# Minus the maximum from one product of four 32-row tiles, and a pair's denominators from one product of four 32-column tiles

## What is computed

```python
q = (c_q @ w_up_q.T).reshape(b, s, H, DH).transpose(0, 2, 1, 3)
k = (c_kv @ w_up_k.T).reshape(b, s, H, DH).transpose(0, 2, 1, 3)
q, k = _apply_rope_subspace(q, DR), _apply_rope_subspace(k, DR)
scores = jnp.einsum('bhqd,bhkd->bhqk', q, k) * scale
attn = jax.nn.softmax(scores, axis=-1)
out = jnp.einsum('bhqk,bhkd->bhqd', attn, v)      # v = c_kv @ w_up_v.T
out = out @ w_out.T + residual
```

## Time and profile before

| | us |
|---|---|
| median of 3 runs | 938.64 |
| fastest and slowest of them | 935.33, 938.98 |
| the profiled execution | 931.6 |
| its span | 929.6 |
| PE busy in the span | 822.2 (88%) |
| DVE busy | 664.6 (71%) |
| POOL busy | 633.4 (68%) |
| ACT busy | 384.8 (41%) |

### The profile page before, as it was taken

One profiled execution on the slowest core, in us unless ns is written; L12 is line 12 of the kernel. 1 busy time (PEld: TensorE's weight loads), 2 busy tenths in 40 slices (PEclk: granted clock), 3 DMA queues, 4 the chain that ended last, 5 costly groups with the idle time before them and its releaser, 6 DMA issues.

```text
span 929.6 us, 14668 instructions
## 1 busy us (share of the span) xinstructions
PE 822.2 (88%) x5118; PEld 493.0 (53%) x5118; DVE 664.6 (71%) x1198; ACT 384.8 (41%) x622; POOL 633.4 (68%) x324
## 2 busy tenths in 40 slices
PE   3555799999999999999999999999999979859681
PEld 2323555555555555555555555555555435448681
DVE  7897877777777777777777777777777776646022
ACT  2203354444444444444444444444444434316350
POOL 3201897878878787878787878787877777432433
PEclk8757799999999999999999999999999999879796
DMA  7200000101010101111010111010010000058693
GB/s 201 65 0 1 12 13 13 25 13 24 13 24 13 25 13 25 26 22 24 13 24 13 24 14 24 13 24 14 13 13 13 13 13 13 12 185 268 214 332 85
DMA packets 84328, 43.88 MB, mean 47 GB/s; under 512 B 57632, under 2 KB 73376, under 8 KB 84192
## 3 DMA queue, kind: packets, MB, share of 16 engines
q1 hardware_dynamic: 83232, 40.86, 17.2%
q0 software_dynamic: 1024, 2.10, 0.8%
HBM read 36.51 MB, written 6.16 MB: 46 GB/s over the span
## 4 chain that ended last, share of the span: by engine, by line
PE 75%; DVE 13%; DMA 4%; issue 2%; POOL 2%; ACT 1%; SPq 1%; POOLq 0%; DVEq 0%
PE ps_o L428 24%; PE ps_m L394 8%; PE ps_x L382 8%; PE ps_s L412 6%; PE ps_s L414 6%; PE ps_s L418 6%; PE ps_s L416 6%; PE ps_s L443 3%; DVE mx L941 3%; DMA moe<-xs_dram 2%; PE ps_s L436 2%; POOL xs_dram L808 2%; PE ps_s L547 1%; PE ps_s L538 1%; DVE hn L878 1%
## 5 line engine op out<-in xcount | busy, mean ns | idle before, releaser
L794 POOL TENSOR_TENSOR acc<-acc,probs 128x1024 f32<-128x1024 f32 (+1 forms) x192 | 460.1, 2396 | 83.2 <-ACT probs L633 61.4
L941 DVE TENSOR_REDUCE mx<-ps_m 128x2 f32<-128x1024 f32 x240 | 293.6, 1223 | 91.6 <-PE ps_m L394 91.1
L633 ACT ACTIVATE probs<-ps_s 128x1024 f32<-128x1024 f32 x256 | 249.2, 1024 | 165.1 <-PE ps_s L418 165.1
L428 PE MATMUL ps_o<-probs,c_all 128*64 128x512 f32 x1024 | 249.7, 609 | 0.0
L394 PE MATMUL ps_m<-k_hi,q_hi 64*128 64x512 f32 x480 | 108.3, 446 | 11.0 <-issue 6.6
L794 POOL TENSOR_TENSOR acc<-probs 128x1024 f32<-128x1024 f32 (+1 forms) x32 | 75.4, 2355 | 58.8 <-ACT probs L633 58.3
L412 PE MATMUL ps_s<-q_hi,k_hi 64*128 64x512 f32 x512 | 103.8, 401 | 11.9 <-DVE x_sb L1005 11.9
L428 PEld LDWEIGHTS ps_o<-probs,c_all 128*64 128x64 f32 x1024 | 62.4, 137 | 93.0 <-issue 43.6
L414 PE MATMUL ps_s<-q_hi,k_lo 64*128 64x512 f32 x512 | 102.7, 396 | 0.0
L418 PE MATMUL ps_s<-neg_row,one_row 64*128 64x512 f32 x512 | 102.1, 393 | 0.0
L416 PE MATMUL ps_s<-q_lo,k_hi 64*128 64x512 f32 x512 | 102.0, 393 | 0.0
(11 more groups left out here) (264 smaller groups left out, 1018.5 us busy)
## 6 DMA issues: line engine op xcount, KB each, us to landing
probs<-in_experts SPq DMA_DIRECT2D x15, 578.0 KB, 5.8
rr<-rd_dram SPq DMA_DIRECT2D x62, 128.0 KB, 3.1
wu<-in_wqk SPq DMA_DIRECT2D x16, 256.0 KB, 3.3
neg_row<-nm SPq DMA_DIRECT2D x256, 0.5 KB, 2.0
w_first<-in_experts SPq DMA_DIRECT2D x5, 578.0 KB, 4.4
rot<-in_experts SPq DMA_DIRECT2D x5, 578.0 KB, 5.7
hT<-in_experts SPq DMA_DIRECT2D x5, 578.0 KB, 5.6
xs_dram<-zero SPq DMA_DIRECT2D x2, 960.0 KB, 6.5
```

The lines of the kernel that those rows point to most:

```text
L428: ins = nc.tensor.matmul(ps_o[64 * h:64 * h + 64, :], c_all[:, (p // HP) * TB + kt, :], probs[:, st % 4, h, :], start=(kt == 0), stop=(kt ...
L633: nc.scalar.activation(probs[:, st % 4, :, :], ps_s[:, 2 * (st % 2):2 * (st % 2) + 2, :], ACT.Exp, scale=SCALE).then_inc(s["probs"], 1)
L794: V.tensor_tensor(acc[:, half, heads, :], first, probs[:, st % 4, heads, :], ALU.add).then_inc(s["added"], 1)
L941: V.reduce_max(mx[:, :, kh, qt], max_banks(q, n), AX.X).then_inc(s["max_reduced"], 1)
```

## The change

Four things are done at once.

1. `less_max(p, g)` comes ahead of the two scores of a group: four matmuls on 32-row tiles (partitions 0, 32, 64, 96), one for each head and step, into the four banks of `ps_s`, which start the accumulation that `score` goes on with. `score` loses its fourth product. `one_row` has ones in four partitions, and `neg_row` minus the maxima of head 0 on partitions 0 and 32 and of head 1 on 64 and 96, so `max_rows` has 16 copies for each half instead of 8. As `less_max` writes all four banks it waits for the probabilities of the step just before, and in group 0 for both output sums of the pair before, in group 4 for the read of the denominators.
2. `denominators(p - 1, (0, 1))` makes both halves of a pair at once, with four 32-column tiles, in group 3 of pair p, ahead of `pv`, into bank 0. `acc` and `ou` get a third buffer so that half 0 can wait.
3. Behind it everything of a pair is done once: one read by ScalarE, four copies in `den_cols`, one `recip`, one `inv_rows`, four copies in `inv_spread`, two `divide` at the end of group 6, both `outputs` in group 7 ahead of `pv` (banks 0 and 1), and both `out_add` at the end of group 7.
4. The last pair keeps two separate halves at its end.

```diff
+            def less_max(p, g):
+                half = g // 4
+                ge(pe, s["probs"], n_step(p, 2 * g) - 1)
+                if g % 4 == 0:
+                    pe.wait_ge(row_placed[half], 256 * (p + 1))
+                if g == 0:
+                    ge(pe, s["out_added"], 2 * (p - 1))
+                if g == 4:
+                    ge(pe, s["den_read"], n_den(p - 1))
+                for h in range(2):
+                    for odd in range(2):
+                        j = quarter(2 * h + odd)
+                        nc.tensor.matmul(ps_s[:, 2 * odd + h, :], one_row[j, :],
+                                         neg_row[j, p % 2, half * HALF:(half + 1) * HALF], start=True, stop=False)
...
-                for h in range(2):
-                    ins = nc.tensor.matmul(bank[h], one_row[rows(h), :], neg_row[rows(h), p % 2, qc], start=False, stop=True)
...
+            def denominators(p, halves, bank):
+                for half in halves:
+                    wait_adds(pe, p, TB * half + TB - 1)
+                    for h in range(2):
+                        ins = nc.tensor.matmul(bank[quarter(2 * half + h), :], ones[:, 0:32], acc[:, buf(p, half), h, :],
+                                               start=True, stop=True)
...
@@ PE, in the loop over groups, behind up() @@
+                    if p > 0 and g in (3, 7):
+                        pe.wait_ge(s["probs"], n_step(p, 2 * g))
+                        if g == 3:
+                            denominators(p - 1, (0, 1), ps_s[:, 0, :])
+                        else:
+                            outputs(p - 1, 0, ps_s[:, 0, :])
+                            outputs(p - 1, 1, ps_s[:, 1, :])
@@ DVE, in the loop over groups @@
-                    if g == 0 and p >= 2:
-                        out_add(p - 2, 1, ps_s[:, 3, :])
-                    if g == 4 and p >= 1:
-                        out_add(p - 1, 0, ps_s[:, 3, :])
+                    if g == 5 and p > 0:
+                        recip(p - 1)
                     if p < LAST:
                         reduce_max(p + 1, 2 * g)
...
-                        if g in (0, 4):
-                            recip(p - 1, g // 4)
-                        if g in (2, 6):
-                            divide(p - 1, g // 4)
+                        if g == 6:
+                            divide(p - 1, 0)
+                            divide(p - 1, 1)
+                        if g == 7:
+                            out_add(p - 1, 0, ps_s[:, 0, :])
+                            out_add(p - 1, 1, ps_s[:, 1, :])
@@ SP, max_rows @@
-                for h in range(2):
+                for j in range(4):
+                    h = j // 2
                     for n in range(4):
-                        row = neg_row[64 * h:64 * h + 1, ...]
+                        row = neg_row[32 * j:32 * j + 1, ...]
@@ SP, in the loop over pairs @@
-                    den_cols(p - 1, 0)
-                    inv_rows(p - 1, 0)
-                    inv_spread(p - 1, 0)
                 if p < LAST:
                     max_rows(p + 1, 0)
                 if p > 0:
-                    den_cols(p - 1, 1)
-                    inv_rows(p - 1, 1)
-                    inv_spread(p - 1, 1)
+                    den_cols(p - 1, (0, 1))
+                    inv_rows(p - 1, (0, 1))
+                    inv_spread(p - 1, (0, 1))
```

More of the change, by code:

```diff
@@ L200, in build @@
             "added_last": "the same for head 1 of the last pair's second half (vector)",
-            "den_product": "half a pair's denominators (tensor)",
-            "den_read": "and read (scalar)",
-            "inverses": "denominators inverted (vector)",
+            "den_product": "a pair's denominators; half of the last pair's (tensor)",
+            "den_read": "and read (scalar, the last half vector)",
+            "inverses": "and inverted (vector)",
             "sums_copied": "latent sums of half a pair are in SBUF (scalar)",
@@ L268, in n_part, with n_den, buf, quarter @@
             return 2 * p + half + 1
+        def n_den(p, half=0):
+            return p + 1 + (half if p == LAST else 0)
+        def buf(p, half):
+            return (2 * p + half) % 3
+        def quarter(j):
+            return slice(32 * j, 32 * j + 32)
         def n_unit(q, u):
@@ L411, in score @@
                 for h in range(2):
-                    nc.tensor.matmul(bank[h], k_hi[rows(h), p % 3, kc], q_hi[rows(h), p % 3, qc], start=True, stop=False)
+                    nc.tensor.matmul(bank[h], k_hi[rows(h), p % 3, kc], q_hi[rows(h), p % 3, qc], start=False, stop=False)
                 for h in range(2):
@@ L506, in _ @@
                             pv(p - 1, NSTEP + n)
[L507 to L518, removed]
             pv(LAST, NSTEP - 2)
             pv(LAST, NSTEP - 1)
-            pe.wait_ge(s["den_read"], n_part(LAST, 0))
-            denominators(LAST, 1, ps_x[:])
+            pe.wait_ge(s["den_read"], n_den(LAST))
+            last_denominators(ps_x[:])
             def slots_T(i, k):
@@ L1250, in max_rows @@
                     sp.wait_ge(s["scores"], n_step(q - 2, TB * half + TB - 1))
[L1251 removed]
+                for j in range(4):
+                    h = j // 2
                     for n in range(4):
[L1253 removed]
+                        row = neg_row[32 * j:32 * j + 1, q % 2, half * HALF + n * P:half * HALF + (n + 1) * P]
                         sp.dma_start(row.bitcast(F32), nm[:, half, h, n:n + 1].bitcast(F32)).then_inc(row_placed[half], 16)
[L1256 to L1262 removed]
@@ L1264, in inv_rows, with den_cols @@
-            def inv_rows(p, half):
-                sp.wait_ge(s["inverses"], 2 * p + half + 1)
-                sp.dma_start(rd_dram[half].rearrange("h (p f) -> p h f", f=4), rc[:, half, :, :]).then_inc(inv_out, 16)
-            def inv_spread(p, half):
-                sp.wait_ge(inv_out, 16 * (2 * p + half + 1))
-                for h in range(2):
-                    sp.dma_start(rr[64 * h:64 * h + 64, half, :],
-                                 rd_dram[half, h:h + 1, :].to_broadcast([64, HALF])).then_inc(inv_in, 16)
+            def den_cols(p, halves):
+                sp.wait_ge(s["den_read"], n_den(p))
+                ge(sp, s["inverses"], p)
+                for half in halves:
+                    for h in range(2):
+                        j = 32 * (2 * half + h)
+                        sp.dma_start(denc[:, half, h, :], den[j:j + 1, :]).then_inc(den_cols_in, 16)
@@ new lines, in inv_rows, with inv_spread @@
+            def inv_rows(p, halves):
+                sp.wait_ge(s["inverses"], p + 1)
+                some = slice(halves[0], halves[-1] + 1)
+                sp.dma_start(rd_dram[some].rearrange("a h (p f) -> p (a h) f", f=4),
+                             rc[:, some, :, :].rearrange("p a h f -> p (a h) f")).then_inc(inv_out, 16)
+            def inv_spread(p, halves):
+                sp.wait_ge(inv_out, 16 * (p + 1))
+                for half in halves:
+                    for h in range(2):
+                        sp.dma_start(rr[64 * h:64 * h + 64, half, :],
+                                     rd_dram[half, h:h + 1, :].to_broadcast([64, HALF])).then_inc(inv_in, 16)
```

100 lines of the change are left out of this document (45 added, 55 removed).

## The result

| | us |
|---|---|
| before, median of 4 runs | 936.99 |
| after, median of 4 runs | 1111.87 |
| fastest and slowest of the 4 after | 1109.56, 1555.98 |
| ratio after / before | 1.185, 95% interval 1.182 to 1.188 |
| profiled execution after, its span | 1113.6, 1111.6 |

One of the four runs after took 1555.98 us for a reason that nothing here shows, and the ratio is taken from the other three, of 1109.56, 1110.17 and 1113.57.

What follows compares the result with a forecast made beforehand. PE was taken as the bound. A middle pair gains 0.5 + 6.2 (queue wait) + 2.5 (clock) = 9.2 us, times 13 is 119.6; with 6.8 + 0.5 - 7 it is +120 on 938.64, forecast 1058 us, range 1015 to 1085.

Steps and rivals of the forecast that it cites:

- The bound and the prices on PE: PE bounds middle pairs, busy all 44.1 us; a tile shape change costs 0.12 to 0.20, a new group takes 5.20.
- free changes: On PE around the four 32-row matmuls: changes between 64 and 32 rows cost nothing, total 1020 us; chance 0.12.
- two by two: On PE in less_max: the four tiles run in twos, 0.46 us a set, total 1080 us; chance 0.05.
- The queue: SyncE's queue: 16 copies at 0.64 us ahead of the denominators' four bring their columns 14.3 us after neg_max.
- The first wait: PE ahead of step 11's maxima stands still 6.2 us in each of pairs 1 to 14.
- the clock: PE works at about half clock behind each new wait and loses 2.5 us, between 0 and 3.4 possible.
- The divides: End of group 6: two divides in a row make VectorE 0.7 us later for group 7's first maximum; 0.2 charged.
- The ends: First and last pairs: pair 14 +6.8 us, pair 0 +0.5, last pair with the tail -7.
- a reciprocal in time: SyncE's queue: twenty issues take 6.0 us, 0.3 each, so the reciprocal isn't late; 935 us, no change; chance 0.04.
- that with free changes: Reciprocal not late and shape changes on PE free: 3.2 us less in each of 15 pairs, 887 us; chance 0.03.
- a longer set: Four 32-row tiles run 3.07 times, not 4: set some 0.1 us longer, about 13 us over 128 groups, left out.

Runs made afterwards that it cites:

- experiment 4: The changed kernel with minus the maximum made by two pairs of 64-row matmuls in the same place, 16 copies kept: 1092.1 us.
- experiment 1: The changed kernel with the denominators' copies, inverses' copy and spread ahead of the 16 copies of maxima in SyncE's list: 976.5 us, ratio 1.048.
- experiment 5: The kernel before with only minus the maximum from four 32-row tiles and 16 copies for a half: 1146.2 us, ratio 1.221.
- experiment 2: The changed kernel with GpSimd adding only 8 of 512 columns in steps 11 to 13 of pairs 1 to 14: 1058.3 us.
- experiment 3: The changed kernel with the two divides of a pair joined into one instruction over 128 x 1024: 1059.2 us.
- experiment 7: The changed kernel with denominators' steps ahead of the copies of maxima and one divide for both halves, four 32-row tiles kept: 946.9 us, ratio 1.010.
- experiment 9: The changed kernel with denominators' steps first, one divide, 64-row tiles for minus the maximum and 8 copies for a half: 917.8 us, ratio 0.983.

## Why the prediction was right or wrong

- **The bound and the prices on PE: right.** 5.22 us for a plain group (5.20 forecast), 6.2 for group 3 (5.20 + 1.01). That a change between 64 and 32 rows costs 0.20 like the others, which no row showed, holds (the 0.43 us on both sides of L421, and experiment 4). The rivals of free changes and of two by two are out.
- **The queue: right in mechanism, size and place.** The first wait is 6.3 us on average over pairs 1 to 13, 6.2 forecast; experiments 1 and 5 show it from two sides. Group 5 as a whole is 14.4 us on average: 5.2, the wait, and 2.9 for the clock and the unhidden start behind the wait, where 2.5 stood.
- **The divides: this step failed.** The prediction has "Two `divide` in a row at the end of group 6 make VectorE 0.7 later for the first maximum of group 7", and charges 0.2, with nothing for the clock. VectorE was 3.0 later: PE waits 2.2 us, and in 11 of the 13 pairs works at half clock behind it. The step priced an instruction by the duration that it had in its old place. Group 7 is 10.9 us on average, not 7.2: 3.7 in each of 13 pairs, 48 of the 54 us by which the 13 middle pairs were under-sized. Experiments 2 and 3 show the cause. The trace of before held a warning: divides there take 0.68 us, but two of them, both in pair 14, take 2.40 and 2.74. The ordinary ones began just as an add of GpSimd ended; these two began 1.85 and 2.19 us before one ended, and end 0.55 us behind it (753.62 against 753.07), as in the changed kernel. Here is the longer of them with the add that it met, of the kernel before:

```profile
750.69 2.38 POOL L794 TENSOR_TENSOR acc<-acc,probs 128x1024 f32<-128x1024 f32 x1
```

```profile
750.88 2.74 DVE L998 TENSOR_TENSOR ou<-ou,rr 128x512 f32<-128x512 f32 x1
```

  And here is a stretch of GpSimd's timeline of the kernel before, with an ordinary divide and the add behind it:

```profile
527.93 4.91 POOL L794 TENSOR_TENSOR acc<-acc,probs 128x1024 f32<-128x1024 f32 x2
```

```profile
532.74 0.68 DVE L998 TENSOR_TENSOR ou<-ou,rr 128x512 f32<-128x512 f32 x1
```

```profile
532.99 2.71 POOL L794 TENSOR_TENSOR acc<-acc,probs 128x1024 f32<-128x1024 f32 x1
```

  Two adds end at 532.84, the divide starts 0.1 before that, and the next add takes 2.71 where these two took 2.4 each: so by its duration it waits for the divide. A second divide right behind finds that add under way. The Trainium skill has this as a rule, which the prediction left out: in SBUF — State Buffer, section SBUF: two separate sides, a VectorE instruction with two SBUF inputs and a GpSimd instruction that reads SBUF want the same pair of ports, the one that starts first has it for the whole instruction, and the other blocks. This case's runs agree: 0.84 and 2.88 us, and 0.68 for all with the adds narrowed. They show who waits for whom; the ports themselves no trace shows.
- **The ends: too large a gain.** The last pair with the tail gave 3.7 us instead of 7, pair 14 cost 8.7 instead of 6.8. The first pair is 1.4 shorter, not 0.5 longer, and the start before it took 5.0 more in the profiled execution; the kernels of the experiments, whose start is the same or nearly so, lie between 0.5 less and 1.9 more there, so I leave that open.
- **Put together** the 13 middle pairs take 173 us more, forecast 120. The forecast of 1058 with the 48 us of the divides is 1106, over the range's upper end of 1085; the measured 1111.87 without them is 1064, inside the range.
- **Two slips in its numbers** change nothing above. It gives 0.04 to a reciprocal in time (no change) and 0.03 to that with free changes (faster), but ends with same 0.03 and faster 0.04. The 13 us that it names for a longer set should be 9, as 0.23 x 4 / 3.07 is 0.07 over 0.23, not 0.1; the trace shows neither, since from the set to the score are 0.43 us, as from the 64-row `maxima` to the set.

## What to carry to other kernels

An in-order DMA queue is an engine like any other: count how long it issues, 0.64 us for a small copy here, and ask who waits for what stands behind. An instruction that is moved next to another of its kind doesn't keep its duration if another engine's long instructions can hold it up: of two VectorE operations in a row with two SBUF inputs each, the second waited out an add of GpSimd that had just begun, while one instruction over both tiles is held up once at most. The longest duration in a group, not only the median, shows such a case before the change is made. Packing small matmuls into more tiles is worth its gain less a change of shape on each side; here 0.23 us saved a group cost 0.40.

## What the runs showed that I had not expected

- A divide of 128 x 512 on VectorE takes 0.68 us alone, 0.84 when the add of GpSimd that it meets has 0.3 left, and 2.88 when it has 2.3 left: some 0.55 more than what is left of the add. Adds of GpSimd stretch from 2.4 to 2.7 in turn.
- A wait of PE of 2.2 us brought a stretch at the 1.2 GHz level behind it in 11 of 13 pairs of the changed kernel, 3.5 us of work in the one shown, but in 6 of 13 in experiment 1, where the wait is as long; why it differs is open. The wait of 7.3 brought 5.4 in the pair shown. With the waits gone (experiments 7 and 9) the granted clock is full (1.00) from pair 2 to pair 13.
- A burst of 16 small copies took 10.1 to 10.2 us to issue in most cases and up to 11.45 in others, where one copy took 1.1 to 1.8 us. Why that one does is open.
